# Causal running sums of the attention scores on one Trainium2 core: reversed score rows, the carry in the last partition, one triangular product

## The reference, cut to what matters

```python
S = relu(att[:, 0])                  # att = q k^T / sqrt(8), causal: key j <= query i
S[..., 0] = 0.0
S = S * (1 - eye(T))                 # the diagonal is cleared
S_shifted = concat([zeros(B, 1, T), S[:, :-1]], axis=1)
FF = cumsum(S_shifted, axis=1)       # FF[i, j] = sum of S[r, j] over the rows r < i
att = att - FF[:, None]              # for all heads
# then per row: keep the 408 smallest FF among the causal keys, softmax, times v
```

## Time and profile before

| what | value |
|---|---|
| runs | 2947.10, 2940.08, 2943.28 us (median 2943.28) |
| the profiled execution | 2941.24 us, of which the span of the profile is 2939.4 us |
| mean granted TensorE clock | 0.952 |
| the q, k, v part | 0 to 26.7 us |
| the running sums | 26.7 to 111.3 us |
| the search of the threshold | from 111.3 us |

### The profile page before, as it was taken

One profiled execution on the slowest core, in us unless ns is written; L12 is line 12 of the kernel. 1 busy time (PEld: TensorE's weight loads), 2 busy tenths in 40 slices (PEclk: granted clock), 3 DMA queues, 4 the chain that ended last, 5 costly groups with the idle time before them and its releaser, 6 DMA issues. The chain is left out here.

```text
span 2939.4 us, 75860 instructions
## 1 busy us (share of the span) xinstructions
PE 2613.1 (89%) x31084; PEld 1634.9 (56%) x31084; DVE 1845.0 (63%) x5185; ACT 1785.3 (61%) x3488; POOL 345.4 (12%) x710
## 2 busy tenths in 40 slices
PE   8998978888889799999998989999999999896596
PEld 4696846666666462212122546766676767665355
DVE  6899977887887572100002657777877777763862
ACT  3585745655666328999997236766666666532331
POOL 3100042222221010000000100000000000016026
PEclk9998989999999899999999999999999999898598
DMA  3320010000010202100000010000000000303003
GB/s 116 57 39 1 2 16 17 17 16 11 11 16 11 53 1 83 54 30 1 1 1 17 1 40 7 2 8 7 2 7 7 7 2 2 97 13 50 29 15 58
DMA packets 85120, 68.23 MB, mean 23 GB/s; under 512 B 40776, under 2 KB 73688, under 8 KB 84392
## 3 DMA queue, kind: packets, MB, share of 16 engines
q1 hardware_dynamic: 76328, 57.09, 7.8%
q0 software_dynamic: 8448, 6.30, 1.5%
HBM read 47.21 MB, written 19.96 MB: 23 GB/s over the span
## 5 line engine op out<-in xcount | busy, mean ns | idle before, releaser
L1746 ACT ACTIVATE arena<-ps 128x1024 f32<-128x1024 f32 x512 | 474.1, 1281 | 25.9 <-PE ps L1696 24.0
L1197 DVE CUSTOM_DVE_ANT_0 arena<-ps,arena 128x1024 f32<-128x1024 f32 (+7 forms) x384 | 349.8, 931 | 107.4 <-PE ps L1073 91.4
L2124 DVE CUSTOM_DVE_ANT_0 arena<-ps,arena 128x512 f32<-128x512 f32 (+3 forms) x640 | 371.1, 643 | 26.7 <-PE ps L1988 25.8
L1149 ACT ACTIVATE arena<-ps 128x1024 f32<-128x1024 f32 (+3 forms) x320 | 275.3, 896 | 133.5 <-PE ps L1106 130.1
L2081 ACT ACTIVATE arena<-arena 128x1152 f32<-128x1152 f32 (+15 forms) x256 | 306.4, 1199 | 63.4 <-DVE arena L2124 63.4
L1988 PE MATMUL ps<-arena 64*128 64x512 f32 (+3 forms) x1280 | 270.4, 547 | 3.5 <-ACT arena L2057 1.1
L1707 PE MATMUL ps<-arena 128*32 128x512 f32 x2048 | 273.0, 604 | 0.0
L2019 PE MATMUL ps<-arena 128*64 128x128 f32 x4352 | 262.3, 275 | 0.0
L2019 PEld LDWEIGHTS ps<-arena 128*64 128x64 f32 x4352 | 235.3, 137 | 33.4 <-issue 28.7
L900 PE MATMUL ps<-arena 128*128 128x256 bf16 (+1 forms) x2176 | 239.0, 274 | 14.7 <-DVE arena L872 9.3
L2043 ACT COPY arena<-ps 128x512 f32<-128x512 f32 (+3 forms) x410 | 189.7, 517 | 75.9 <-PE ps L2005 73.7
(11 more groups left out here) (298 smaller groups left out, 4056.6 us busy)
## 6 DMA issues: line engine op xcount, KB each, us to landing
arena<-scr_q SPq DMA_DIRECT2D x256, 32.0 KB
scr_s<-scr_f SPq DMA_DIRECT2D x1, 4096.0 KB, 16.3
arena<-scr_k SPq DMA_DIRECT2D x32, 128.0 KB
arena<-by_head_k SPq DMA_DIRECT2D x16, 192.0 KB
arena<-scr_s SPq DMA_DIRECT2D x16, 192.0 KB, 2.5
arena<-by_head_q SPq DMA_DIRECT2D x28, 96.0 KB
by_head_k<-arena SPq DMA_DIRECT2D x5, 512.0 KB, 4.5
scr_x<-arena SPq DMA_DIRECT2D x2, 1024.0 KB, 5.3
```

The costliest lines, as they stand in the source:

```text
L1149: e.activation(turned_block(u, kc), src, ACT.Exp, scale=-1.0).then_inc(exped, 1)
L1197: e.tensor_tensor_reduce(scored_block(u, g)[:, lo:hi], PS[:, 1024 * (k % 2):1024 * (k % 2) + hi - lo], NF[t][:, lo:hi], -1.0, mxs[:, col - ...
L1746: e.activation(PTR[k % RS], PS[:, at(n):at(n) + 1024], ACT.Sigmoid, scale=float(1 / np.sqrt(8.0))).then_inc(weighed, 1)
L2124: e.tensor_tensor_reduce(slot(u, t, g)[:, lo:hi], PS[:, base(step) + 512 * g:base(step) + 512 * g + hi - lo], bias, -1.0, mxs[:, col - 1:c ...
```

## The change

The score rows of a tile are turned round and moved up by one: partition p of tile t now holds row 128t + 126 - p, and partition 127 holds row 128t - 1, the last row of the tile in front. Row 127 of `NF[t-1]` is the running sum up to, and without, that row. It is added onto partition 127 of the score rows (a product with a 0/1 column `LAST`, taken over partitions 96 to 127), and then one product with the turned triangle `UP` (1 where k + m >= 127) gives all of `NF[t]`. `cacc`, its addition, and the product with ones are gone. To turn the scores, q's eight rows are copied by GpSimd in reversed order within each tile into `q_rows`, whose other groups are then filled from there. The masks of the scores get other bounds and cover one column more. The close of tile t now also waits for the last carry taken from `NF[t]`, so `take_high` comes a tile later in VectorE's list. The carries of a tile, one for each chunk of the tile in front (36 in all), stand at the head of the tile's work on VectorE.

```diff
@@ qkv_sync
-                    for ready, of, to in ((3 * c + 1, q_t, q_rows), (3 * c + 3, k_t, k_rows)):
-                        w.wait_ge(qkv_biased, ready)
+                    for by, ready, of, to in ((filled, 7 + c, q_rows, q_rows), (qkv_biased, 3 * c + 3, k_t, k_rows)):
+                        w.wait_ge(by, ready)
@@ qkv_gpsimd
                 e.memset(V9, 1.0).then_inc(filled, 1)
-                e.memset(cacc, 0.0).then_inc(filled, 1)
-            cacc = reg(AT + 4096, 2048)
+                e.memset(reg(ST - 1, 1), 0.0).then_inc(filled, 1)
+                e.memset(UP, 1.0).then_inc(filled, 1)
+                e.memset(LAST, 1.0).then_inc(filled, 1)
+                w.wait_ge(filled, 4)
+                e.affine_select(out=UP, in_=UP, compare_op=ALU.is_ge, fill=0.0,
+                                base=-127, pattern=[[1, 128]], channel_multiplier=1).then_inc(filled, 1)
+                e.affine_select(out=LAST, in_=LAST, compare_op=ALU.is_ge, fill=0.0,
+                                base=-127, pattern=[[0, 1]], channel_multiplier=1).then_inc(filled, 1)
+            UP, LAST = reg(AT + 4096, 128), SM[:, 720:721]
@@ head_rows
-                return (q_t[rows], k_t[rows]) if g == 0 else (q_rows[rows], k_rows[rows])
+                return q_rows[rows], k_t[rows] if g == 0 else k_rows[rows]
+            carries = [(t, i) for t in range(1, NT) for i in range(len(pieces_of[t - 1]))]
+            carry_no = {x: n for n, x in enumerate(carries)}
@@ sums_tensor
                         w.wait_ge(qkv_biased, 3 * (t // 4) + 3)
+                        w.wait_ge(filled, 7 + t // 4)
...
                         w.wait_ge(f_masked, 2 * t + 2)
-                        i = c0 // 512
-                        if t and i < len(pieces_of[t - 1]):
-                            w.wait_ge(f_carry, pieces_of[t - 1][i] + 1)
+                        if (t, c0 // 512) in carry_no:
+                            w.wait_ge(f_carry, carry_no[t, c0 // 512] + 1)
                         else:
-                            w.wait_ge(filled, 2)
+                            w.wait_ge(filled, 6)
...
-                        e.matmul(bank(4 + n % 4, c1 - c0), LST, srow[t % 3][:, c0:c1], start=True, stop=False)
-                        e.matmul(bank(4 + n % 4, c1 - c0), ONE, cacc[:, c0:c1], start=False, stop=True).then_inc(f_summed, 1)
+                        e.matmul(bank(4 + n % 4, c1 - c0), UP, srow[t % 3][:, c0:c1], start=True, stop=True).then_inc(f_summed, 1)
@@ sums_scalar
                         if t >= 3:
-                            w.wait_ge(f_carry, upto[t - 3])
+                            w.wait_ge(f_summed, upto[t - 3])
@@ sums_gpsimd
+                    lo = max(128 * t - 1, 0)
+                    block = sr[:, lo:128 * t + 128]
                     w.wait_ge(f_relu, upto[t])
-                    e.affine_select(out=tile(sr, t), in_=tile(sr, t), compare_op=ALU.is_gt, fill=0.0,
-                                    base=0, pattern=[[-1, 128]], channel_multiplier=1).then_inc(f_masked, 1)
+                    e.affine_select(out=block, in_=block, compare_op=ALU.is_ge, fill=0.0,
+                                    base=125 + 128 * t - lo, pattern=[[-1, 128 * t + 128 - lo]], channel_multiplier=-1).then_inc(f_masked, 1)
...
+                for c in range(4):
+                    x = q_t[0:8, 512 * c + 126:512 * c + 127]
+                    w.wait_ge(qkv_biased, 3 * c + 1)
+                    e.tensor_copy(cols(q_rows, c)[0:8, :].rearrange("p (t x) -> p t x", t=4), bass.AP(x.tensor, x.offset, [x.ap[0], [128, 4], [-1, 128]])).then_inc(filled, 1)
                 masked(0)
...
                     w.wait_ge(f_copied, upto[t])
+                    if t + 1 < NT:
+                        w.wait_ge(f_carry, carry_no[t + 1, len(pieces_of[t]) - 1] + 1)
@@ carry (new), sums_vector
+            def carry(e, w, t, i):
+                lo, hi = 512 * i, min(512 * i + 512, 128 * t)
+                n = pieces_of[t - 1][i]
+                last = srow[t % 3][96:128, lo:hi]
+                w.wait_ge(f_copied, n + 1)
+                w.wait_ge(f_masked, 2 * t + 2)
+                e.scalar_tensor_tensor(last, NF[t - 1][96:128, lo:hi], LAST[96:128, :], last, ALU.mult, ALU.add).then_inc(f_carry, 1)
...
-                for n, (t, c0, c1) in enumerate(chunks):
-                    w.wait_ge(f_summed, n + 1)
-                    w.wait_ge(f_masked, 2 * t + 2)
-                    if t and c0 // 512 < len(pieces_of[t - 1]):
-                        w.wait_ge(f_carry, pieces_of[t - 1][c0 // 512] + 1)
-                    e.tensor_tensor(cacc[:, c0:c1], cacc[:, c0:c1], srow[t % 3][:, c0:c1], ALU.add).then_inc(f_carry, 1)
-                    if c1 < 128 * (t + 1):
-                        continue
+                for t in range(NT):
+                    if t:
+                        for i in range(len(pieces_of[t - 1])):
+                            carry(e, w, t, i)
...
-                    if t >= 4:
-                        take_high(e, w, t - 1)
+                    if t >= 5:
+                        take_high(e, w, t - 2)
                     if 4 <= t < 14:
                         split(e, w, t - 4)
+                take_high(e, w, 14)
                 take_high(e, w, 15)
@@ attend_sync
-                w.wait_ge(f_carry, len(chunks))
+                w.wait_ge(f_summed, len(chunks))
```

More of the change, by code:

```diff
@@ L787, in sums_gpsimd @@
                     w.wait_ge(f_copied, upto[t])
+                    if t + 1 < NT:
+                        w.wait_ge(f_carry, carry_no[t + 1, len(pieces_of[t]) - 1] + 1)
                     e.affine_select(out=tile(NF[t], t), in_=tile(NF[t], t), compare_op=ALU.is_ge, fill=BIG,
                                     base=0, pattern=[[-1, 128]], channel_multiplier=1).then_inc(f_closed, 1)
-            def sums_vector(e, w):
-                w.wait_ge(filled, 2)
-                for n, (t, c0, c1) in enumerate(chunks):
-                    w.wait_ge(f_summed, n + 1)
-                    w.wait_ge(f_masked, 2 * t + 2)
-                    if t and c0 // 512 < len(pieces_of[t - 1]):
-                        w.wait_ge(f_carry, pieces_of[t - 1][c0 // 512] + 1)
-                    e.tensor_tensor(cacc[:, c0:c1], cacc[:, c0:c1], srow[t % 3][:, c0:c1], ALU.add).then_inc(f_carry, 1)
-                    if c1 < 128 * (t + 1):
-                        continue
+            def carry(e, w, t, i):
[5 more added lines that the diff above has]
+                e.scalar_tensor_tensor(last, NF[t - 1][96:128, lo:hi], LAST[96:128, :], last, ALU.mult, ALU.add).then_inc(f_carry, 1)
+            def sums_vector(e, w):
+                w.wait_ge(filled, 6)
+                for t in range(NT):
+                    if t:
+                        for i in range(len(pieces_of[t - 1])):
+                            carry(e, w, t, i)
                     if t == 3:
```

## The result

The changed kernel takes 2931.01 us (median of 6 runs, 2924.89 to 2931.73) against 2946.06 us of the kernel before (median of 6); the ratio is 0.9945, with a 95% interval of 0.9933 to 0.9957. That is 15.1 us less; the forecast was 18.2 less, and 2925.

A forecast was written before the change was run, and what follows sets the result against it. TensorE bounds the sums now; VectorE was to become the bound. Bias on X at 38.4 plus 51.4 us, then the tail, puts the search at 92.8, not 111.0: 18.2 us less, forecast 2925, range 2917 to 2936.

The forecast's parts named there:

- The bound moves from TensorE to VectorE: In the sums stage VectorE ends last, at 89.8 us against TensorE's 77.8, and is the new bound.
- the sum: VectorE's instructions from the bias on X at 38.4 us to tile 13's high half at 89.8: 51.4 us.
- carries: VectorE's 33 carries of tiles 4 to 15: 21.1 us; 32 partitions priced like 128, 512 columns at 0.75.
- the tail: Stage end after tile 13's high half: last copy, close and high half, from 89.8 us to the search at 92.8.
- The front: Before the bias on X: GpSimd's reversed copy 0.75 us, rows ready at 35.4, bias starts at 38.4, not 41.75.
- tile 2 at half clock: Tile 2's single product on TensorE, start 35.8 us, copy from 37.3, within 3.5 us at half clock.
- one wait, carry of tile 4 for tile 3's sum and copy: 0.3: After the bias on X, VectorE waits just once for a carry's input, 0.3 us.
- the last entry: GpSimd's selects slow the next VectorE instruction by 0.1 us each, two in each of 12 tiles: 1.4 us net.
- rival 3: Idle gaps in each tile keep TensorE at 1.2 GHz through the sums: slower, 2951 us; chance 0.04.
- at half clock TensorE would be full again, and full it got its clock back: Argument against TensorE staying at 1.2 GHz in the sums; a full TensorE had recovered after 3.5 us.
- rival 2: GpSimd locked out by saturated VectorE, masks delay carries: 6.6 to 13 us, say 10; 2935 us; chance 0.17.
- Rival 1: TensorE stays the bound in the sums because VectorE's work costs less: search at 80.3, 2913 us; chance 0.05.

The follow-up runs named there:

- the last pair of runs: Changed kernel plus one 256-column extra product before each sum of tiles 2 to 7, over 128 rows or 8 rows: 2944.46 and 2960.08 us.
- the 8-row run: Changed kernel plus one 256-column extra product over 8 rows before each sum product of tiles 2 to 7: 2960.08 us, search start 113.2.
- sixth experiment: Changed kernel plus extra products in the row wait (five) and before sums of tiles 2 to 7, four splits moved before 37 us: 2917.85 us, ratio 0.9911.
- third experiment: Kernel before the change without the product with ones, carry left out of the sums, cacc additions kept: ratio 0.9941, search start 98.1.
- second experiment: Changed kernel plus four 512-column extra products in the row wait and one of 256 before each sum of tiles 2 to 7: ratio 0.9946.

## Why the prediction was right, and what was wrong in it

**The bound moves from TensorE to VectorE: right,** from 62 us on in the changed kernel, and in the whole stretch once the clock was up. With the clock at full speed for all but 3 to 7 us of the stretch the sum holds to half a microsecond: 54.1 measured against 54.4 from X to the search. Its terms hold too: carries 0.75 us on 32 partitions, as priced from 128; the tail 3.1 for 3.0. The front was 0.4 us early only by the 0.8 us of head start; tile 2 at half clock cost 0.5 more than reckoned.

**The term that failed** is "one wait, carry of tile 4 for tile 3's sum and copy: 0.3". There were eight waits of 6.4 us together. With them the stretch from X to tile 13's high half is 56.7 us; without them 50.3, 0.8 less than the 51.1 of VectorE's work in the sum. That difference is in the direction of the last entry, GpSimd's selects at 1.4, for which the run without closes shows much less.

**The step behind it** is in rival 3: "at half clock TensorE would be full again, and full it got its clock back". The first half was right, the second wrong. In the rows I argued from, TensorE did tile 2's pair of products over all 128 rows from 34.94 on the earlier trace rows. After the change a larger share of its time is score products over 8 rows: 2.0 of the 4.4 us from 40.72 to 45.16, in the kernel before 1.1 of the 3.4 from 41.03 to 44.44. TensorE was full from 38 to 62 and stayed at 1.2 GHz. That this share is the reason is what the last pair of runs speaks for; it is not shown beyond them. So the half clock of rival 3 was there, though not its reason: for 29 us instead of the whole stage, and without idle gaps in the tiles. It cost 6 us and not more because TensorE had slack against VectorE, as the forecast said of short drops; the 8-row run comes close to the rival's end (search at 113.2, the rival had 119.1). That the total stayed in the range is in part luck: the range was widened for rival 2, and nothing in the sum bounded how long the clock would stay at half. The second rule of the Trainium skill that I weighed (TensorE: Matmul & The Clock Gate, A second HAM failure mode: psum-queue depth-cycling) speaks of short idles. The short drop at 75 does come behind an idle time of 1.27 us; in the long one the traces show a clock at half from 38 to 62 while the records have no idle time at all. I gave the rival 0.04, too little.

**Rival 2, GpSimd locked out: not seen.** Its masks were never what a carry waited for; all of VectorE's waits for carries were for copies. The first rule of the Trainium skill (SBUF - State Buffer, Who interferes with whom), which for two SBUF inputs speaks of GpSimd instructions that read SBUF, as a select does, fits the changed kernel: a select held up by VectorE ended about one instruction later (70.64 + 2.38 = 73.02, the memset behind it at 73.24), and no select of the changed kernel took over 2.34 us, of its variants over 2.41. It does not explain the 5.71 us of the kernel before, which no run here reproduced; that stays open.

**Rival 1, TensorE the bound: wrong for the change from 62 us on, right where the splits were taken away** (tiles 8 to 10 of the sixth experiment).

**Noise.** 13.2 us of the 15.1 are seen in the stage. The rest lies within the interval of the ratio (0.9933 to 0.9957 is 12.7 to 19.7 us).

## What to carry to other kernels

When a change takes work off the bounding engine, add up the next engine's queue instruction by instruction; here it gave the new length to half a microsecond, once the clock was up. Then look at what clock the lighter TensorE is granted: here the products that stayed ran at half clock for 29 us, and that cost 6 us of waits. Extra products over all 128 rows in its waits and ahead of the sums, and movable work put where the new bound is idle, together took another 10 us off the stage (search at 98.3 and 87.9 on the same chip).

## What the runs showed that I had not expected

- Without the product with ones the clock fell earlier and stayed down. In the two traces with it, it fell at 35.0 and 34.3, behind the idle time, and was back after 3.4 us. In the ten without it, it fell between 28.9 and 31.0, with the loop (the change and its variants) and without it (third experiment); in six of them while TensorE was still at score products. So the wait for the rows did not bring the fall in those six. Where no extra products followed, it was back at 61.2 to 61.7 in all four traces.
- TensorE can be busy by the records for 24 of 24 us and stay at 1.2 GHz. Extra 256-column products over 128 rows brought it back at 47.4 us, the same over 8 rows not before 83.4.
- Extra products in the wait did not prevent the fall, but the clock was back sooner. With four of 512 columns from 31.19 on (6.61 us) it was back at 37.1; with the same four from 31.23 on (5.14 us, the run without closes) at 34.2; with five of 256 from 30.43 on (3.88 us) at 33.4. Two executions with the same products lie 3 us apart, so these times do not tell which number or moment is best. In the run without closes the clock fell again at 41.0 and stayed at half to 54.7; with extra products in tiles 2 to 7 as well (second experiment and both remedies) it held beyond 62.
